# First and last iterations of a two-layer attention pipeline rebuilt, the mask moved behind the projection, new instruction orders

## Chip, cores, metric

The kernel runs on one core of a Trainium2 chip. The metric is the device time of one execution in microseconds (us), lower is better. TensorE is written PE, VectorE DVE, ScalarE ACT, GpSimd POOL, SyncE SP.

## What is computed

For each of 16 batches `x` is 256 x 512 (features x time) and `mask` is one row of 512 values of 0 or 1. All arrays are fp32. Cut to what matters:

```python
def layer0(x, mask):                       # 8 heads of 32
    q = transpose(x) @ Wq.T                # 512 x 256; keys and values are q as well
    logits = (scale * q q^T * cmask + (1 - cmask) * NEG) * rmask
    ctx = softmax(logits) @ q              # a masked query row gets the plain mean of q over time
    return transpose(ctx @ Wo.T)

def layer1(x, emb=mask):                   # 16 heads of 32, rows are the 256 features
    scale, shift = split(emb @ W_emb + b_emb)
    xn = rms_norm(x) * g_norm * (1 + scale) + shift
    q, k, v = xn @ W_qkv;  q, k = rms_norm over each head of 32
    o = softmax(q k^T * 32**-0.5) @ v
    return o + o @ W_out

x = x + layer0(x, mask);  x = x + layer1(x, mask)
```

## The kernel before

Every engine has its own instruction list, written out by hand; semaphores tie the lists. `pipeline` runs i from -1 to 17. Iteration i of every engine works on three batches at once: layer 0 of batch i, layer 1 of batch i-1, the last output steps of batch i-2, and the projection of batch i+1. Iterations -1, 0, 15, 16 and 17 have lists of their own, 1 to 14 share `iteration`. Iterations 2 to 14 have all four parts; below they are called full iterations. The tables `BIG`, `MAXES`, `CONTEXT_TAKEN`, `VISITS` and `SCORES` hold the order in which steps use a PSUM bank, and every wait count is computed from them.

Layer 0 of a batch. SP loads `XB` (x) and `CBM` (the mask on all partitions) in `load_x`. DVE sums x over time (`sums_x`, L1559), POOL multiplies x by the mask (`mask_x`, L1935; in the first batch DVE does, L1554). PE projects in two halves mt (`project0`, L398) into bank PX; ACT copies to `QF` (`take_query`) and rounds to `QHI` (`round_query`); DVE makes the rest `QLO` (`split0`). PE also projects the sums (`project_mean`, L406: 4 matmuls of one column), and ACT scales that to `MEAN` (L1078). SP stacks high and low parts into `A0` and `B0` (`stack0`, 6 DMAs per head, 64 KB each, L2093), so that one matmul gives near-fp32 scores. PE makes scores once to find row maxima (`maxima0`, L422; DVE reduces, L1565), transposes the maxima (`rows0`, L437), ACT copies them and sends them by DMA into row 96 of `B0` (L1092). Then come 32 scores (`score0`, L453), 32 exponentials (L1048), sums over keys on POOL and DVE, values times weights (`values_weighted0`, L480), sums through a matmul with ones (L491), reciprocals, the mean for masked rows (`context0`, L1614), the output matmul (`out0`, L519), residual, RMS norm, transposes (`norm_rows`, L530) and modulation (`modulate`, which needs `AMOD` and `SMOD`).

Layer 1 of a batch. PE projects in four pieces of 4 matmuls (`qk`, L541) through the one bank PX; ACT copies (`take_heads`) and squares (`square_heads`), DVE sums and adds eps, POOL raises to the power -0.5 (`power_heads`, L1960) and multiplies (`norm_heads`, L1967); PE transposes (`heads_rows`, L559), ACT rounds, DVE splits, SP stacks (`stack1`, 6 DMAs per group of heads, 128 KB each), PE and DVE find maxima (`maxima1`, L431 and L1572), all 32 rows are transposed together (`rows1`, L441) and sent by one DMA. The value projection (`values1`, also L541) and 16 steps of scores (`score1`, L467), exponentials (L1055), `values_and_sums1` (L502, L505) and the output (`out1`, L575) follow, and SP stores. `score1` of the first group waits for `row1_in`, the landing of the row of maxima.

Start. ACT waits for WQ and x, then issues nine loads (`loads`), then its first activation. PE computes the modulation for all batches in iteration -1 (`modulation(n)`, L374, 8 calls of 4 matmuls of 16 columns into PO), in pieces between the maxima of batch 0; `WEMB` lies inside the buffer `E` of the exponentials. SP stacks all heads of batch 0.

End. Iteration 16 has only layer 1 of batch 15. PE's four `qk` pieces take turns with ACT's copies of bank PX; the stacks go out on SP alone:

```python
def iteration_16(i):           # SP
    stack1(i, i - 1, 0)
    stack1(i, i - 1, 1)
    stack1(i, i - 1, 2)
    stack1(i, i - 1, 3)
    store(i, i - 2)
```

## Times and profile before

| | us |
|---|---|
| three runs | 1325.32, 1330.34, 1330.52; median 1330.34 |
| profiled execution | 1324.62 |
| its span | 1322.8 |
| PE busy in the span | 1261.4 (95%) |
| DVE / ACT / POOL busy | 1055.8 / 774.6 / 764.4 |

The profiled execution is one further run; its span is from the first to the last instruction, and 1.8 us lie around it. Busy time is the union of an engine's instructions. The granted clock of TensorE has the mean 0.972 over the span; it is either full (2.4 GHz, 1.0) or half (1.2 GHz, 0.5) at a time.

### The profile page before, as it was taken

The page shows a single profiled execution, that of the slowest core. Times are in us where ns is not written, and L with a number is a line of the kernel's source. Part 1 is how long each engine was busy: PE and PEld are TensorE (multiplying, and loading weights), DVE is VectorE, ACT ScalarE, POOL GpSimd, SP SyncE. Part 2 cuts the span into 40 slices and gives each one's busy share as a digit, 9 for nine tenths or more (in the row PEclk, how much of TensorE's full clock was granted, in tenths as well). Part 3 has the DMA queues.
Part 4 walks back from the last instruction along what each step waited for, and adds up shares of the span by engine and source line. Part 5 has one row for each costly group of instructions (what it writes and reads, how often), then busy time and mean ns, then how long its engine had stood idle before and what let it go on. Part 6 is the DMA issues. An engine that isn't in the chain of part 4 may idle for free.

```text
span 1322.8 us, 20986 instructions
## 1 busy us (share of the span) xinstructions
PE 1261.4 (95%) x6896; PEld 597.6 (45%) x6896; DVE 1055.8 (80%) x934; ACT 774.6 (59%) x1377; POOL 764.4 (58%) x389
## 2 busy tenths in 40 slices
PE   6969899999999999999999999999999999999987
PEld 4424444444444454444445444444444444444433
DVE  6756778888887887888788788878888887888654
ACT  1626565665656566565656666565666656566523
POOL 0337467475746747484674748467474856638452
PEclk8859899999999999999999999999999999999999
DMA  8321534525264452626445252634525263441322
GB/s 288 105 65 47 136 105 96 140 54 151 74 148 109 99 138 56 149 72 150 107 107 131 60 147 70 153 104 112 130 60 145 69 156 100 113 110 44 97 59 70
DMA packets 77962, 143.03 MB, mean 108 GB/s; under 512 B 21536, under 2 KB 23072, under 8 KB 77856
## 3 DMA queue, kind: packets, MB, share of 16 engines
q1 hardware_dynamic: 69136, 126.17, 38.1%
q10 hardware_dynamic: 8720, 15.51, 4.0%
q8 instruction: 59, 0.97, 0.3%
q14 instruction: 47, 0.39, 0.1%
HBM read 32.02 MB, written 8.39 MB: 31 GB/s over the span
## 4 chain that ended last, share of the span: by engine, by line
PE 88%; ACT 4%; DVE 2%; issue 2%; SPq 1%; ACTq 1%; POOL 1%; DMA 0%; DVEq 0%
PE PX L541 25%; PE PS L453 11%; PE PO L480 9%; PE PX L575 8%; PE PO L502 5%; PE PS L467 4%; PE PX L398 4%; PE PM L422 4%; PE PX L519 2%; PE PM L491 2%; PE PM L519 2%; PE PM L559 2%; PE PM L431 2%; PE PO L505 2%; ACT E L1055 2%
## 5 line engine op out<-in xcount | busy, mean ns | idle before, releaser
L1048 ACT ACTIVATE E<-PS,KBIAS 128x512 f32<-128x512 f32 x512 | 345.3, 686 | 236.8 <-PE PS L453 221.9
L541 PE MATMUL PX<-WQKV,XNT 128*128 128x512 f32 x768 | 382.4, 602 | 3.4 <-ACT QK L1026 2.1
L1948 POOL TENSOR_TENSOR E<-E 128x1024 f32<-128x1024 f32 x112 | 263.4, 2359 | 160.8 <-PE PO L480 92.9
L1565 DVE TENSOR_REDUCE NM<-PM 128x4 f32<-128x2048 f32 x128 | 291.3, 2276 | 52.3 <-PE PM L422 52.3
L453 PE MATMUL PS<-B,A 97*128 97x512 f32 x512 | 301.7, 624 | 5.3 <-ACT E L1048 4.9
L1978 POOL TENSOR_TENSOR KQLO<-E 128x1024 f32<-128x1024 f32 x64 | 151.2, 2363 | 211.3 <-ACT E L1055 209.5
L1960 POOL TENSOR_TENSOR RQK<-RQK,HALF 128x16 f32<-128x16 f32 x64 | 201.0, 3148 | 28.3 <-DVE RQK L1653 27.5
L1572 DVE TENSOR_REDUCE NM<-PM 128x8 f32<-128x2048 f32 x64 | 146.6, 2291 | 49.1 <-PE PM L431 49.0
L541 PEld LDWEIGHTS PX<-WQKV,XNT 128*128 128x128 f32 x768 | 137.8, 192 | 91.4 <-issue 75.7
L1055 ACT ACTIVATE E<-PS 128x512 f32<-128x512 f32 x256 | 145.3, 596 | 49.0 <-PE PS L467 48.3
L453 PEld LDWEIGHTS PS<-B,A 97*128 97x128 f32 x512 | 95.6, 192 | 148.1 <-issue 123.6
L480 PE MATMUL PO<-E,V 128*32 128x512 f32 x1024 | 139.5, 617 | 0.0
L467 PE MATMUL PS<-B,A 97*128 97x256 f32 x512 | 124.4, 350 | 8.8 <-ACT E L1055 8.2
L1672 DVE RECIPROCAL T<-T 128x256 f32<-128x256 f32 x64 | 111.5, 1742 | 12.4 <-ACT T L1026 12.4
L575 PE MATMUL PX<-WOUT,OT 128*128 128x512 f32 x248 | 120.5, 605 | 0.0
L467 PEld LDWEIGHTS PS<-B,A 97*128 97x128 f32 x512 | 77.2, 188 | 80.2 <-issue 53.1
L1603 DVE RECIPROCAL R<-R 128x256 f32<-128x256 f32 x64 | 109.8, 1736 | 1.1
L1583 DVE TENSOR_TENSOR E<-E 128x1024 f32<-128x1024 f32 x80 | 97.7, 1238 | 11.9 <-ACT E L1048 10.1
L1935 POOL TENSOR_TENSOR XB<-XB,CBM 128x512 f32<-128x512 f32 x30 | 37.8, 1281 | 72.6 <-DVE XS L1559 56.6
L422 PE MATMUL PM<-QHI 32*128 32x512 f32 x512 | 67.1, 513 | 10.5 <-DVE NM L1565 6.9
L1646 DVE TENSOR_REDUCE SSQ<-YSQ 128x16 f32<-128x512 f32 x64 | 42.8, 669 | 40.2 <-ACT YSQ L1116 40.1
L398 PE MATMUL PX<-XB,WQ 128*128 128x512 f32 x128 | 65.6, 637 | 8.0 <-DVE XB L1554 8.0
(84 smaller groups left out, 1408.2 us busy)
## 6 DMA issues: line engine op xcount, KB each, us to landing
A<-QHI SPq DMA_DIRECT2D x256, 64.0 KB, 2.0
B<-QHI SPq DMA_DIRECT2D x256, 64.0 KB, 2.0
A<-KQHI SPq DMA_DIRECT2D x128, 128.0 KB, 2.3
B<-KQHI SPq DMA_DIRECT2D x128, 128.0 KB, 2.4
XB<-x SPq DMA_DIRECT2D x16, 512.0 KB, 3.9
A<-QLO SPq DMA_DIRECT2D x128, 64.0 KB, 2.0
B<-QLO SPq DMA_DIRECT2D x128, 64.0 KB, 2.0
X<-x ACTq DMA_DIRECT2D x16, 512.0 KB, 5.4
```

What stands on the lines that cost most here:

```text
L453: mm(PS[n % 2][:, :], A0[0:97, h, g * P:(g + 1) * P], B0[0:97, h, :], start=True, stop=True).then_inc(score_full, 1)
L467: last = mm(PS[n % 2][:, kb * N1:(kb + 1) * N1], A1[0:97, hq, c, kb * P:(kb + 1) * P], B1[0:97, hq, c, :], start=True, stop=True)
L480: last = mm(PO[h * DH:(h + 1) * DH, :], V0[:, q, g, h * DH:(h + 1) * DH], E[:, probs(seg, i, g), h, :], start=(g == 0), stop=(g == KB0 - 1))
L541: last = mm(PX[:, :], XNT[:, c, t * P:(t + 1) * P], WQKV[:, c, part * DM:(part + 1) * DM], start=(c == 0), stop=(c == 3))
L575: last = mm(bank, OT[:, c, t * P:(t + 1) * P], WOUT[:, c, :], start=(c == 0), stop=(c == 3))
L1048: fn(E[:, probs(seg, i, g), h, :], PS[n % 2][:, :], ACT.Exp, bias=KBIAS[:, g, b:b + 1], scale=SCALE).then_inc(exp_done, 1)
L1055: fn(E[:, probs("C", i, c), h, :], PS[n % 2][:, :], ACT.Exp, scale=SCALE_RAW).then_inc(exp_done, 1)
L1565: v.tensor_reduce(NM0[:, q, :].rearrange("p (h k) -> p h k", k=KB0)[:, :, kb], PM[:, :, :], axis=AX.X, op=ALU.max, negate=True).then_inc(m ...
L1572: v.tensor_reduce(NM1[:, :].rearrange("p (h c a) -> p h c a", c=Q1, a=2)[:, :, c, :], PM[:, :, :].rearrange("p h (a k) -> p h a k", a=2), ...
L1948: g_.tensor_tensor(running(seg, i)[:, heads_, :], running(seg, i)[:, heads_, :], E[:, probs(seg, i, g), heads_, :], ALU.add).then_inc(done, 1)
L1960: g_.tensor_tensor(rqk, rqk, HALF[:, :], ALU.pow).then_inc(rqk_done.sem, 1)
L1978: g_.tensor_tensor(key_sums(c), e[:, :, 0:N1], e[:, :, N1:2 * N1], ALU.add).then_inc(esum_done.sem, 1)
```

## The change

- **Mask after the projection.** x is projected as it is. `take_query` also gives the sum of its input over time (`accum_out` into `QSUM`), which replaces `sums_x` (DVE), `project_mean` (PE) and `mean0` (ACT); the factor 1/512 goes into `CBI` and into NEG. POOL multiplies `QF` by the mask (`mask_query`, two multiplications per batch as before), and `round_query` and the transposes of `values0` wait for it.
- **Start.** ACT issues five small loads and waits for nothing before them. SP issues the large ones: W_emb and W_o behind the first stack, W_qkv and W_out behind the last stack of iteration -1. ACT issues four of the eight stacks of batch 0. `WEMB` has space of its own under `B1` and what follows. The modulation is one block in iteration 0, into PX, between scores; DVE's part of it and `residual_weights` are in iteration 0 too.
- **Full iterations.** All engines but SP get a new order: `qk`, `out1`, `maxima1` and `values1` are cut and spread otherwise, `heads_rows` come earlier, `split0` of the second half and `round_query` of it come at the end, `masked_out` stands behind the fourth `power_heads`.
- **Iteration 15** has new orders; the store comes behind the stacks.
- **Iteration 16.** The odd `qk` pieces go through bank 3 of PM. `norm_heads` is on DVE. ACT issues two of the four stacks, SP the others. The maxima are transposed and sent in two halves (`rows1_half`), four DMAs each, and scores of groups 0 and 1 wait only for the first half.

```diff
-            def project_mean(i, b):
-                big(("mean", 0), i)
-                pe.wait_ge(xs_done.sem, xs_done.at(b))
-                for mt in range(2):
-                    for c in range(2):
-                        last = mm(PX[:, mt:mt + 1], WQ[:, c, mt * P:(mt + 1) * P], XS[:, c:c + 1],
-                                  start=(c == 0), stop=(c == 1))
-                last.then_inc(p0_full.sem, 1)
...
             def project0(i, b, mt):
-                pe.wait_ge(xm_done.sem, xm_done.at(b))
+                pe.wait_ge(xin_in.sem, xin_in.at(b))
...
+            def rows1_half(i, b, j):
+
+                pe.wait_ge(context_taken, CONTEXT_TAKEN.ahead(("n1", j), i))
+                pe.wait_ge(max_done, MAXES.upto(("c", 2 * j + 1), i, QUAD))
+                tp(PO[0:H1, j * P:(j + 1) * P], NM1[:, j * H1:(j + 1) * H1], IDENT[:, :]).then_inc(n1_half[j], 1)
...
             def score1(i, b, c, hq):
...
+                if b == NB - 1:
+                    if u in (0, 8):
+                        pe.wait_ge(row1_half_in[u // 8], 16 * QH)
+                elif u == 0:
...
         @block.scalar
...
-                copy(QF[:, mt, :], PX[:, :]).then_inc(big_taken, 1)
+                fn(QF[:, mt, :], PX[:, :], ACT.Copy, accum_out=QSUM[:, mt, b:b + 1]).then_inc(big_taken, 1)
...
             def round_query(i, b, mt):
-                act.wait_ge(big_taken, BIG.upto(("p0", mt), i))
+                act.wait_ge(masked.sem, masked.at(b, mt + 1))
...
+            def rows1_half(i, b, j):
+                act.wait_ge(n1_half[j], 1)
...
+                copy(NMT1[0:H1, j, :], PO[0:H1, j * P:(j + 1) * P]).then_inc(context_taken, 1)
+                act.wait_ge(context_taken, CONTEXT_TAKEN.upto(("n1", j), i))
+                for h in range(QH):
+                    act.dma_start(B1[96:97, h, 2 * j:2 * j + 2, :].rearrange("p c (k t) -> p (c k) t", t=P).bitcast(F32),
+                                  NMT1[h * QH:(h + 1) * QH, j, :].bitcast(F32)).then_inc(row1_half_in[j], 16)
...
             def loads():
-                act.wait_ge(wq_in.sem, 16)
-                act.wait_ge(xin_in.sem, xin_in.at(0))
...
         @block.gpsimd
...
-            def mask_x(i, b):
+            def mask_query(i, b, mt):
                 pool.wait_ge(cbm_in.sem, cbm_in.at(b))
-                pool.wait_ge(xs_done.sem, xs_done.at(b))
-                for c in range(2):
-                    g_.tensor_tensor(XB[:, c, :], XB[:, c, :], CBM[:, :], ALU.mult).then_inc(xm_done.sem, 1)
+                pool.wait_ge(big_taken, BIG.upto(("p0", mt), i))
+                g_.tensor_tensor(QF[:, mt, :], QF[:, mt, :], CBM[:, :], ALU.mult).then_inc(masked.sem, 1)
...
         @block.sync
...
             def iteration_before(i):
-                stack0(i + 1, 0, 3)
-                stack0(i + 1, 0, 1)
                 stack0(i + 1, 0, 0)
+                load_modulation()
                 load_x(i + 2)
                 stack0(i + 1, 0, 2)
-                stack0(i + 1, 1, 3)
                 stack0(i + 1, 1, 2)
                 stack0(i + 1, 1, 0)
-                stack0(i + 1, 1, 1)
+                load_weights()
...
             def iteration_16(i):
                 stack1(i, i - 1, 0)
-                stack1(i, i - 1, 1)
-                stack1(i, i - 1, 2)
-                stack1(i, i - 1, 3)
                 store(i, i - 2)
+                stack1(i, i - 1, 2)
```

How the rows move is shown at three places. First PE from its first instruction to the third piece of batch 0's scores (PX<-XB,WQ is `project0`, PM<-QHI `maxima0`, PO<-CT,E or PX<-CT,WEMB the modulation, IDENT,NM `rows0`, IDENT,QF `values0`, PS<-B,A the scores). Before:

```order
1 L398 MATMUL PX<-XB,WQ 128x512 x2
2 L422 MATMUL PM<-QHI 128x512 x4
3 L398 MATMUL PX<-XB,WQ 128x512 x2
4 L422 MATMUL PM<-QHI 128x512 x4
5 L374 MATMUL PO<-CT,E 128x16 x12
6 L422 MATMUL PM<-QHI 128x512 x8
7 L374 MATMUL PO<-CT,E 128x16 x4
8 L406 MATMUL PX<-XS,WQ 128x1 x4
9 L437 MATMUL PM<-IDENT,NM 16x128
10 L374 MATMUL PO<-CT,E 128x16 x16
11 L414 MATMUL PM<-IDENT,QF 128x128 x4
12 L453 MATMUL PS<-B,A 128x512 x2
```

Now:

```order
1 L427 MATMUL PX<-XB,WQ 128x512 x4
2 L442 MATMUL PM<-QHI 128x512 x16
3 L457 MATMUL PM<-IDENT,NM 16x128
4 L434 MATMUL PM<-IDENT,QF 128x128 x4
5 L427 MATMUL PX<-XB,WQ 128x512 x2
6 L442 MATMUL PM<-QHI 128x512 x4
7 L479 MATMUL PS<-B,A 128x512 x4
...
15 L479 MATMUL PS<-B,A 128x512 x2
16 L442 MATMUL PM<-QHI 128x512 x4
17 L411 MATMUL PX<-CT,WEMB 128x16 x32
18 L457 MATMUL PM<-IDENT,NM 16x128
```

The 32 modulation matmuls left the stretch ahead of the first score and stand behind the twelfth, and half of batch 1's projection and a piece of maxima stand ahead of the first.

Second PE in a full iteration, from the end of the first quarter of scores to the first `maxima1` (IDENT,QK is `heads_rows`, PM<-KQHI `maxima1`, PX<-WOUT,OT `out1`). Before:

```order
475 L398 MATMUL PX<-XB,WQ 128x512 x2
476 L453 MATMUL PS<-B,A 128x512 x2
477 L559 MATMUL PM<-IDENT,QK 128x128 x8
478 L398 MATMUL PX<-XB,WQ 128x512 x2
479 L453 MATMUL PS<-B,A 128x512
480 L491 MATMUL PM<-E,ONES 32x512 x4
481 L453 MATMUL PS<-B,A 128x512 x2
482 L559 MATMUL PM<-IDENT,QK 128x128 x8
483 L453 MATMUL PS<-B,A 128x512 x2
484 L480 MATMUL PO<-E,V 32x512 x4
485 L406 MATMUL PX<-XS,WQ 128x1 x4
486 L431 MATMUL PM<-KQHI 128x256 x8
```

Now:

```order
477 L427 MATMUL PX<-XB,WQ 128x512 x2
478 L593 MATMUL PM<-IDENT,QK 128x128 x8
479 L479 MATMUL PS<-B,A 128x512 x2
480 L427 MATMUL PX<-XB,WQ 128x512 x2
481 L518 MATMUL PM<-E,ONES 32x512 x4
482 L479 MATMUL PS<-B,A 128x512 x2
483 L593 MATMUL PM<-IDENT,QK 128x128 x8
484 L479 MATMUL PS<-B,A 128x512
485 L507 MATMUL PO<-E,V 32x512 x4
486 L609 MATMUL PX<-WOUT,OT 128x512
487 L479 MATMUL PS<-B,A 128x512
488 L451 MATMUL PM<-KQHI 128x256 x8
```

The row with XS is gone, and both blocks of `heads_rows` stand ahead of scores that they stood behind.

Third ACT in iteration 16, from the rounding of keys and queries to the exponentials of group 1 (NMT are the maxima, V the values). Before:

```order
984 L1132 ACTIVATE KQHI<-PM,GQK 128x512 x4
985 L1026 ACTIVATE V<-PX 128x512
986 L1026 ACTIVATE NMT<-PM 32x128
987 L1100 DMA B<-NMT 1x32x128
988 L1055 ACTIVATE E<-PS 128x512 x6
```

Now:

```order
952 L1184 ACTIVATE KQHI<-PM,GQK 128x512 x4
953 L1098 DMA A<-KQHI 32x1024
...
962 L1098 DMA B<-KQLO 32x1024
963 L1055 ACTIVATE NMT<-PO 16x128
964 L1148 DMA B<-NMT 1x4x128 x4
965 L1055 ACTIVATE V<-PX 128x512
966 L1084 ACTIVATE E<-PS 128x512 x4
967 L1055 ACTIVATE NMT<-PO 16x128
968 L1148 DMA B<-NMT 1x4x128 x4
969 L1084 ACTIVATE E<-PS 128x512 x2
```

Twelve stack DMAs stand ahead of the maxima, and the second half of the maxima, with four DMAs, stands between exponentials.

## Rows read from the trace of the kernel before

**Rows 1.** The page, part 1: engine, busy us (share of the span), instructions.

```profile
PE 1261.4 (95%) x6896; PEld 597.6 (45%) x6896; DVE 1055.8 (80%) x934; ACT 774.6 (59%) x1377; POOL 764.4 (58%) x389
```

**Rows 2.** Busy time by stretch, with granted clock, DMA share, GB/s.

```profile
0.00:35.90 35.90, 22.96 (x97) 16.77 (x98) 20.98 (x17) 4.18 (x7) 0.73 (x7) 0.79 0.85 279
35.90:99.70 63.80, 49.62 (x188) 20.39 (x189) 41.57 (x41) 27.92 (x50) 22.82 (x12) 0.69 0.31 81
99.70:178.60 78.90, 73.86 (x389) 34.66 (x387) 58.47 (x52) 47.49 (x85) 45.40 (x23) 0.92 0.39 94
178.60:1179.30 1000.70, 987.04 (x5559) 467.46 (x5555) 845.06 (x742) 627.74 (x1118) 621.60 (x312) 1.00 0.44 110
1179.30:1252.70 73.40, 70.44 (x398) 32.43 (x395) 54.70 (x50) 45.25 (x79) 46.16 (x22) 1.00 0.31 78
1252.70:1310.90 58.20, 48.72 (x244) 22.33 (x242) 27.46 (x28) 20.87 (x37) 25.98 (x13) 0.94 0.27 64
```

**Rows 3.** Timeline of PE, full iteration: start us, us, instruction, [idle before <-releaser].

```profile
444.58 1.05 PE L406 MATMUL PX<-XS,WQ 128*128 128x1 f32 x8
445.56 0.51 PE L431 MATMUL PM<-KQHI 32*128 32x256 f32 x8
```

**Rows 4.** Timeline of PE near the end of the same iteration.

```profile
479.19 0.50 PE L467 MATMUL PS<-B,A 97*128 97x256 f32 x2 [0.45 <-ACT E L1055]
...
482.52 0.28 PE L437 MATMUL PM<-IDENT,NM 128*16 128x128 f32 x1 [0.29 <-DVE NM L1565]
...
485.05 1.07 PE L502 MATMUL PO<-E,V 128*32 128x256 f32 x16 [0.29 <-ACT T L1026]
```

**Rows 5.** Timeline of POOL in the same iteration: mask, powers, normalised heads.

```profile
425.92 0.62 POOL L1939 TENSOR_SCALAR CBI<-CBI 128x512 f32<-128x512 f32 x1 [0.52 <-DMA CBI<-cond]
...
436.99 3.81 POOL L1960 TENSOR_TENSOR RQK<-RQK,HALF 128x16 f32<-128x16 f32 x1 [0.36 <-DVE RQK L1653]
440.88 1.05 POOL L1967 TENSOR_TENSOR QK<-QK,RQK 128x512 f32<-128x512 f32 x1
```

**Rows 6.** Timeline of PE there: the second block of `heads_rows`.

```profile
441.98 1.09 PE L559 MATMUL PM<-IDENT,QK 128*128 128x128 f32 x8
```

**Rows 7.** Timeline of PE in iteration 1, layer 1 maxima and what follows.

```profile
142.22 0.51 PE L431 MATMUL PM<-KQHI 32*128 32x256 f32 x8 [1.96 <-DVE NM L1572]
...
145.12 0.80 PE L431 MATMUL PM<-KQHI 32*128 32x256 f32 x8 [0.81 <-DVE NM L1572]
...
148.65 1.94 PE L480 MATMUL PO<-E,V 128*32 128x512 f32 x8
```

**Rows 8.** Timeline of PE at the start.

```profile
8.01 3.75 PE L398 MATMUL PX<-XB,WQ 128*128 128x512 f32 x4 [8.01 <-DVE XB L1554]
...
29.26 6.85 PE L374 MATMUL PO<-CT,E 128*128 128x16 f32 x32
...
36.69 1.20 PE L453 MATMUL PS<-B,A 97*128 97x512 f32 x2
```

**Rows 9.** Timeline of ACT at the start (ACTq: its DMA issues).

```profile
12.89 0.60 ACT L1026 ACTIVATE QF<-PX 128x512 f32<-128x512 f32 x1
...
29.80 0.60 ACTq L1092 DMA_DIRECT2D B<-NMT  x1
```

**Rows 10.** Timeline of PE in iteration 16.

```profile
1256.99 3.70 PE L541 MATMUL PX<-WQKV,XNT 128*128 128x512 f32 x8 [0.69 <-ACT QK L1026]
...
1297.18 0.71 PE L467 MATMUL PS<-B,A 97*128 97x256 f32 x4 [0.51 <-issue]
```

**Rows 11.** Timeline of SP's issues in iteration 16, first and last of 24.

```profile
1278.93 0.51 SPq L2093 DMA_DIRECT2D A<-KQHI  x1
...
1294.71 0.59 SPq L2093 DMA_DIRECT2D B<-KQLO  x1
```

**Rows 12.** Timeline of ACT in iteration 16.

```profile
1294.42 0.53 ACTq L1100 DMA_DIRECT2D B<-NMT  x1
```

**Rows 13.** DMA issues over the run: KB each, median us to landing.

```profile
A<-KQHI SPq DMA_DIRECT2D x128, 128.0 KB, 2.3
```

810 lines of the change are left out of this document (425 added, 385 removed), and 23 rows, old and new, of tables (BIG, special).

## Prediction

> **What bounds the kernel now.** I began with busy time on the page: PE is busy for 1261.4 of 1322.8 us, DVE for 1055.8, ACT and POOL for less than 780 [rows 1]. So PE sets the time, and 61.4 us of the span are its idle time. The table of stretches says where they lie [rows 2]: the 13 full iterations take 1000.7 us, 77.0 each, and PE idles for 13.7 us in all of them, 1.05 each, at a clock of 1.00. The start idles for 12.9, iteration 0 for 14.2, iteration 1 for 5.0, iteration 15 for 3.0, iteration 16 for 9.5. The same rows hold a second loss. A mean clock of 0.69 over iteration 0's 63.8 us is 2 x 0.31 x 63.8 = 40 us at half clock; 0.92 in iteration 1 is 12.6 us, 0.94 in iteration 16 is 7.0 us. Work takes twice as long there, so these cost some 20, 6.3 and 3.5 us.
>
> Then I took PE's timeline for each place that the diff touches. What PE still loses in a full iteration are waits of 0.45, 0.29 and 0.29 us near its end [rows 4]; all else there is work that only fewer instructions can shorten.
>
> **Full iterations, mask after the projection.** Removed on PE: the matmuls of the sums. From their start at 444.58 to the next instruction at 445.56 they hold PE for 0.98 us [rows 3]; PE is the bound, so all of it is gained: **-0.98** each. The sums on DVE, the scaling on ACT and the two masks on POOL go, shrink or stay, on engines with 20 to 42% to spare [rows 1], so I price them at nothing; their cover is PE's work.
>
> **Full iterations, the new order.** It can at most take away the three waits, 1.03 us; a wait can also be hidden in what rows count as busy, so I allow 0.3 more: -1.3. What may come in their place lies on POOL. Before, `masked_out` (0.62 us at 425.92) stood ahead of the powers; the fourth power ran at 436.99 for 3.81 us, the last `norm_heads` from 440.88 to 441.93 [rows 5], and PE began the `heads_rows` that need it at 441.98 [rows 6]. There was no slack. Now 0.62 us of `masked_out` stand between that power and that norm, and PE has less to do before it. So a wait of 0.6 to 1.0 us is born ahead of the second `heads_rows`; I take 1.0. Reorder -1.3, new wait +1.0, sum **-0.3**. With the mask that is -1.3 for each iteration, 13 x 1.3 = **-17**. Ends: -26 (no new wait, 2.0 each beside rounding) and 0 (waits eat what the matmuls gave).
>
> **Start and iteration 0.** Before, PE started at 8.01, released by DVE's masking [rows 8]. Two products of that shape cost 1.05 each on POOL [rows 5], so PE starts some 2 to 3 us earlier. The row of maxima of the first head was issued at 29.80 on ACT [rows 9]; with a landing of 2.3 as the stacks have [rows 13] it was there at 32.1. The first score came only at 36.69, for 16 matmuls of the modulation, which hold PE for 6.85 us from 29.26, stood ahead of it [rows 8]. ACT now has about six issues each of four stacks ahead of that row, 0.6 us each, some 14 us in all, which begin after `round_query`; its own first activation was at 12.89 [rows 9] and moves forward by the 2 to 3 us. That leaves the row at about 30 and the first score at about 32: -4.6. But all 32 modulation matmuls now lie inside iteration 0: 13.7 us at half clock (twice the 6.85), 6.9 at full; I take 10.3. They fill idle time, of which iteration 0 has 14.2 [rows 2]; I count 4 of it. And half of batch 1's projection (3.75 us at half clock [rows 8]) is done before the first score, in time that was idle. -4.6 + 10.3 - 4 - 3.8 = **-2**. Ends: -9 (the modulation wholly in idle time and at full clock) and +8 (nothing filled, clock as before).
>
> **Iteration 1.** PE waited 1.96 and 0.81 for DVE's maxima of layer 1, and the block behind them, 8 passes of 512 columns, took 1.94 us at half clock [rows 7]. The maxima are now spread between other work. The two waits are 2.8; of the 6.3 us that half clock costs, a share goes too. I take **-4**, ends -8 and 0.
>
> **Iteration 15.** It idles for 3.0 us [rows 2]; new orders and the lacking L406 can give half of that: **-1.5**, ends -3 and +1.
>
> **Iteration 16.** Three `qk` pieces wait 0.69 us each for ACT's copy of the one bank [rows 10]; with a second bank these go: -2.1. The 24 stack issues run from 1278.93 to 1295.3 on SP alone [rows 11], 16.4 us, 0.68 each. The maxima row was issued at 1294.42 [rows 12]; it lands 2.3 later and releases the first score at 1297.18 [rows 10]. Now ACT issues 12 stacks ahead of it, from 1276.8 on: 12 x 0.62 = 7.4, then a copy, four DMAs of 0.6, 2.3 of landing, and a remainder for waits: about 1289.6, 7.6 earlier. Given back: the second half's four DMAs (2.4) and its copy stand between exponentials on ACT, and value matmuls that used to fill the wait are left over behind it; 3.1 together. So **-4.5**, ends -2 and -8.5.
>
> Here a rule of the Trainium skill can be set against the rows. The rows say that issue is the bound there: 24 issues fill 16.4 us, and each stack lands 2.3 us after its issue. The Trainium skill (DMA: Bandwidth & Descriptors, Issuing engines are not separate DMA queues) says that DMAs from several engines share the same 16 DMA engines, and issuing from more than one saves only issue time. By rows, 24 x 128 KB in 8.2 us would be 384 GB/s, while the start moved 279 GB/s at a share of 0.85 [rows 2], so at most 328; by that rule the stacks take 9.6 us, and iteration 16 gives 1.4 us less.
>
> **Sum.** -17 - 2 - 4 - 1.5 - 4.5 = -29 against the profiled execution's 1324.62: 1295.6. The runs shown have a median 5.7 us above it, with one of them at 1325.3. I put the forecast a little under half of that above the sum: **1298**, against a median of 1330.3, -2.4%.
>
> **Rivals.**
>
> *A, the chain through POOL is the bound of a full iteration.* For: no slack between norm and `heads_rows` [rows 5, 6], and POOL's powers are long. If the wait is 2.3 us instead of 1.0, the full iterations give nothing: 1324.6 - 12 = 1312.6, and with the allowance for the median 1315. Against: POOL is busy for 58% only [rows 1]. Chance 0.18.
>
> *B, more is hidden than rows show.* Waits that look like work go as well, full iterations take 75 us (-26), and the clock stays full in iteration 1 and most of iteration 0 (-17 instead of -6, from the 26 us that half clock costs): 1324.6 - 26 - 17 - 6 = 1276, with the allowance 1278. For: half clock in iterations 0 and 1 begins behind idle time. Chance 0.12.
>
> *C, slower: a gap in each full iteration that takes the clock down.* In iteration 1, waits of 1.96 and 0.81 close together were followed by half clock: 8 passes took 1.94 us [rows 7] where 0.97 would do. If the new order's `heads_rows` wait and a wait for maxima behind it come to 2 or 3 us within a few us, each full iteration may lose half of some 10 us, as iteration 1 lost 6.3. That is +5 x 13 = 65, less the 29: 1360. [...] Chance 0.04. The Trainium skill (TensorE: Matmul & The Clock Gate, HAM oscillation — how this bites in real kernels) describes this case: a gap that comes once per loop lowers the clock anew each time. Iteration 1's rows agree with it; no full iteration's do.
>
> *D, the change is of no effect where it aims.* The DMAs bound start and end (share 0.85 in the start [rows 2]), the waits in full iterations move instead of going, and only some 5 us of the 12.7 of removed matmuls are left: 1320 to 1325. Chance 0.03.
>
> **How the numbers follow.** Forecast 0.63, A 0.18, B 0.12, C 0.04, D 0.03. The range is the forecast's own, whose ends I add half-way, since they don't fall together: 1281 to 1316. It takes in A, and leaves out most of B, C and D. About 0.5%, 6.6 us, is what a measurement of this kernel can tell from no change. Slower by more: C, 0.04. Within: D and the tail of A, 0.05. Faster: the rest, 0.91.
>
> **What would show it.** Full iterations of 75.7 us; the waits of rows 4 gone; a wait for POOL's QK of 0.6 to 1.0 us ahead of the second `heads_rows`. The first score at about 32 us, and iteration 0 about 2 us longer than before in itself, measured from there. No wait over 1 us for NM in iteration 1. In iteration 16, `qk` without waits and the first score some 22 us behind the end of the last `qk` piece instead of 27.7 [rows 10]. I am wrong if the full iterations stay at 77 us (A), if their clock is below 1.00 (C), or if the gain sits in the first and last iterations.

## Result and the profile after

| | us |
|---|---|
| changed kernel, six runs | 1315.93 to 1320.96; median 1316.75 |
| kernel before, six runs beside it | 1324.55 to 1331.37; median 1330.34 |
| ratio | 0.9923, 95% interval 0.9898 to 0.9948 |
| profiled execution, changed kernel | 1315.93 (span 1313.8) |

The change gives 13.6 us by the medians, and 8.7 between the two profiled executions (1324.62 and 1315.93). Forecast were 1298 and a range from 1281 to 1316, so the time lies just outside it, and the gain is less than half of the forecast one. One execution of a kernel below (mod_late) took 1421.4 us at a mean granted clock of 0.83 and is left out of its median and ratio.

The page of the changed kernel, part 1, answers to [rows 1]:

```profile
PE 1238.3 (94%) x6769; PEld 578.4 (44%) x6769; DVE 1040.7 (79%) x920; ACT 768.5 (58%) x1394; POOL 770.5 (59%) x387
```

PE is busy for 23 us less, DVE for 15 less, but the span is only 9 us shorter: idle time of PE has grown by 14 us. Where, the table by stretch says. For both kernels the stretches end at the same events: the first score of layer 0 of batches 0, 1, 2 and 15, and the first score of iteration 16. Columns as in [rows 2]: stretch, its length, busy time of PE, weight loads, DVE, ACT and POOL, granted clock, DMA share, GB/s. Before:

```profile
0.00:36.70 36.70, 23.76 (x102) 17.57 (x102) 21.53 (x21) 4.18 (x7) 0.73 (x7) 0.79 0.84 275
36.70:103.40 66.70, 52.52 (x195) 22.12 (x194) 43.14 (x41) 28.29 (x50) 24.05 (x14) 0.68 0.32 82
103.40:180.80 77.40, 72.36 (x388) 33.63 (x387) 58.52 (x50) 47.72 (x85) 46.31 (x24) 0.93 0.40 100
180.80:1180.30 999.50, 985.84 (x5548) 466.47 (x5546) 843.89 (x741) 627.74 (x1118) 620.42 (x313) 1.00 0.44 110
1180.30:1297.20 116.90, 106.29 (x526) 47.40 (x524) 76.16 (x74) 54.64 (x95) 63.45 (x31) 0.97 0.32 78
1297.20:1322.80 25.60, 20.61 (x146) 10.38 (x146) 12.59 (x10) 12.08 (x22) 9.48 (x4) 1.00 0.09 34
```

The changed kernel:

```profile
0.00:37.20 37.20, 14.27 (x37) 5.13 (x38) 18.86 (x11) 5.47 (x11) 4.52 (x10) 0.72 0.72 200
37.20:112.10 74.90, 57.31 (x241) 29.00 (x241) 48.13 (x46) 27.36 (x48) 20.13 (x12) 0.71 0.29 97
112.10:188.30 76.20, 70.64 (x381) 32.30 (x380) 55.88 (x48) 47.08 (x86) 46.77 (x24) 0.93 0.41 96
188.30:1171.90 983.60, 970.67 (x5444) 452.80 (x5443) 826.25 (x729) 621.83 (x1131) 628.47 (x313) 1.00 0.45 112
1171.90:1284.10 112.20, 100.42 (x520) 46.09 (x518) 78.80 (x79) 54.43 (x95) 61.15 (x27) 0.98 0.35 88
1284.10:1313.80 29.70, 25.01 (x153) 13.07 (x153) 12.79 (x10) 12.29 (x23) 9.48 (x4) 0.90 0.05 19
```

The 13 full iterations took 999.5 and take 983.6 us, 15.9 less. Iteration 1 is 1.2 shorter. Start and iteration 0 together took 103.4 and take 112.1, 8.7 more. The end, from batch 15's first score of layer 0 on, took 142.5 and takes 141.9, 0.6 less; inside it the first score of iteration 16 comes 4.7 us earlier and the stretch behind it is 4.1 us longer. The sum is the 9.0 us by which the span is shorter.

**Full iterations.** The summary of PE's waits over these 13 iterations (releaser, us in total, times, longest), before:

```profile
PE PS L467 <- ACT E L1055: 5.9, 13, 0.5
PE PO L502 <- ACT T L1026: 3.9, 13, 0.3
PE PM L437 <- DVE NM L1565: 3.8, 13, 0.3
```

and of the changed kernel:

```profile
PE PM L593 <- POOL QK L2013: 10.6, 13, 0.8
```

The three waits of [rows 4] are gone (for ACT's E 0.7 us in total are left), and one new wait of 0.8 us each stands ahead of the second `heads_rows`. POOL's timeline in one iteration shows what makes it, where [rows 5] had the power and the norm back to back:

```profile
441.84 3.81 POOL L2006 TENSOR_TENSOR RQK<-RQK,HALF 128x16 f32<-128x16 f32 x1 [0.33 <-DVE RQK L1693]
445.63 0.62 POOL L1985 TENSOR_SCALAR CBI<-CBI 128x512 f32<-128x512 f32 x1
446.22 1.04 POOL L2013 TENSOR_TENSOR QK<-QK,RQK 128x512 f32<-128x512 f32 x1
```

**Start.** PE begins at 5.66, not at 8.01 [rows 8], as forecast. ACT issues the row of maxima at 29.42 [rows 9]. Then, on PE's timeline:

```profile
31.30 3.78 PE L427 MATMUL PX<-XB,WQ 128*128 128x512 f32 x4 [0.72 <-DMA XB<-x]
35.01 0.80 PE L442 MATMUL PM<-QHI 32*128 32x512 f32 x4
37.21 1.19 PE L479 MATMUL PS<-B,A 97*128 97x512 f32 x2 [1.40 <-issue]
...
50.58 11.11 PE L411 MATMUL PX<-CT,WEMB 128*128 128x16 f32 x64
...
88.17 1.94 PE L518 MATMUL PM<-E,ONES 128*32 128x512 f32 x8 [5.41 <-DVE E L1623]
```

and among the DMA issues between 12 and 45 us (KB each, median us to landing):

```profile
WEMB<-w_emb SPq DMA_DIRECT2D x1, 2048.0 KB, 10.3
A<-QHI ACTq DMA_DIRECT2D x8, 64.0 KB, 6.5
XB<-x SPq DMA_DIRECT2D x1, 512.0 KB, 13.2
B<-NMT ACTq DMA_DIRECT2D x1, 8.0 KB, 7.7
```

The row of 8 KB needed 7.7 us to land (3.6 before) and x of batch 1 13.2 us. SP issued the 2 MB of W_emb at 16.76, ahead of both. W_emb had landed at 27.1, before the row was issued; what was still under way then were x and the stacks, which took 6.5 us to land on ACT's queue and 10.6 on SP's. The modulation, 32 matmuls of 16 columns, holds PE for 11.1 us between scores.

DVE's part of the modulation costs more than its own time. It stands ahead of a reciprocal that POOL needs, and POOL's sums over keys are what DVE's last sums, and so PE at 88.17, wait for:

```profile
73.79 5.54 DVE L1597 TENSOR_SCALAR AMOD<-AMOD,GN 128x16 f32<-128x16 f32 x4
81.06 1.29 POOL L2000 TENSOR_TENSOR QK<-QK,R 128x512 f32<-128x512 f32 x1 [1.90 <-DVE R L1643]
```

**End.** ACT in iteration 16, from its last stack issues on:

```profile
1267.43 0.55 ACTq L1098 DMA_DIRECT2D A<-KQHI  x1
...
1277.54 0.27 ACT L1055 ACTIVATE NMT<-PO 16x128 fp32r<-16x128 f32 x1 [11.07 <-issue]
1277.83 3.00 ACTq L1148 DMA_DIRECT2D B<-NMT  x4
1280.94 0.60 ACT L1055 ACTIVATE V<-PX 128x512 f32<-128x512 f32 x1 [3.14 <-issue]
```

Its 12 issues take from 1267.43 to 1277.44, 0.83 each, where SP's took 0.68 in [rows 11] and I had put 0.62. PE had the maxima of the first half transposed at 1273.7; ACT's copy of them had to wait until 1277.54. PE stood idle for 6.89 us ahead of its first score at 1284.07, fell to half clock, and still had half of the value projection left, which it then made between scores.

### The profile page after: what moved, and what is told of

It is laid out like the page before. It is cut to its first block, busy times and chain, and to the rows that moved or that the text cites. A ratio compares the mean times of both kernels' runs of the same rounds, so it can differ in the third digit from the quotient of the medians.

```text
span 1313.8 us, 20726 instructions
## 1 busy us (share of the span) xinstructions
PE 1238.3 (94%) x6769; PEld 578.4 (44%) x6769; DVE 1040.7 (79%) x920; ACT 768.5 (58%) x1394; POOL 770.5 (59%) x387
## 4 chain that ended last, share of the span: by engine, by line
PE 76%; POOL 8%; issue 4%; DVE 4%; SPq 3%; ACT 2%; DMA 2%; ACTq 1%; POOLq 0%; DVEq 0%
PE PX L575 24%; PE PS L479 8%; PE PO L507 7%; PE PX L609 6%; PE PS L496 6%; POOL RQK L2006 5%; PE PO L529 5%; PE PM L442 4%; SPq L2162 2%; PE PX L546 2%; PE PM L546 2%; PE PO L532 2%; PE PM L451 2%; DMA XB<-x 1%; PE PM L434 1%
## 5 line engine op out<-in xcount | busy, mean ns | idle before, releaser
L1077 ACT ACTIVATE E<-PS,KBIAS 128x512 f32<-128x512 f32 x512 | 340.3, 686 | 193.5 <-PE PS L479 148.8
L575 PE MATMUL PX<-WQKV,XNT 128*128 128x512 f32 x752 | 375.0, 602 | 0.1
L479 PE MATMUL PS<-B,A 97*128 97x512 f32 x512 | 286.6, 598 | 5.3 <-ACT E L1077 3.6
L2006 POOL TENSOR_TENSOR RQK<-RQK,HALF 128x16 f32<-128x16 f32 x64 | 213.6, 3344 | 89.9 <-DVE RQK L1693 89.8
L575 PEld LDWEIGHTS PX<-WQKV,XNT 128*128 128x128 f32 x752 | 133.9, 191 | 96.0 <-issue 86.3
L1612 DVE TENSOR_REDUCE NM<-PM 128x8 f32<-128x2048 f32 x64 | 146.5, 2289 | 37.2 <-PE PM L451 37.2
L496 PE MATMUL PS<-B,A 97*128 97x256 f32 x512 | 138.0, 376 | 9.1 <-issue 6.9
L609 PE MATMUL PX<-WOUT,OT 128*128 128x512 f32 x248 | 125.7, 600 | 0.1
L1623 DVE TENSOR_TENSOR E<-E 128x1024 f32<-128x1024 f32 x80 | 101.8, 1274 | 19.8 <-ACT E L1077 16.6
L1055 ACT ACTIVATE QK<-PX 128x512 f32<-128x512 f32 x62 | 37.1, 599 | 79.3 <-PE PX L575 79.3
L1686 DVE TENSOR_REDUCE SSQ<-YSQ 128x16 f32<-128x512 f32 x64 | 43.7, 683 | 37.9 <-ACT YSQ L1168 37.8
```

Of the source, the lines that this page charges most:

```text
L479: mm(PS[n % 2][:, :], A0[0:97, h, g * P:(g + 1) * P], B0[0:97, h, :], start=True, stop=True).then_inc(score_full, 1)
L496: last = mm(PS[n % 2][:, kb * N1:(kb + 1) * N1], A1[0:97, hq, c, kb * P:(kb + 1) * P], B1[0:97, hq, c, :], start=True, stop=True)
L575: last = mm(bank, XNT[:, c, t * P:(t + 1) * P], WQKV[:, c, part * DM:(part + 1) * DM], start=(c == 0), stop=(c == 3))
L609: last = mm(bank, OT[:, c, t * P:(t + 1) * P], WOUT[:, c, :], start=(c == 0), stop=(c == 3))
L1077: fn(E[:, probs(seg, i, g), h, :], PS[n % 2][:, :], ACT.Exp, bias=KBIAS[:, g, b:b + 1], scale=SCALE).then_inc(exp_done, 1)
L1612: v.tensor_reduce(maxima_rows(b)[:, c // 2, c % 2, :, :], PM[:, :, :].rearrange("p h (a k) -> p h a k", a=2), axis=AX.X, op=ALU.max, negat ...
```

## Experiments

All are edits to the changed kernel and compute what it computes; `sums_back` and `no_slack` add matmuls whose result is overwritten. Stage times of the profiled executions, in us, with the same events as above (full: mean of 13 iterations):

| kernel | first score | iteration 0 | 1 | full | to first score of 16 | tail | median | ratio to before |
|---|---|---|---|---|---|---|---|---|
| before | 36.7 | 66.7 | 77.4 | 76.88 | 116.9 | 25.6 | 1330.3 | |
| changed | 37.2 | 74.9 | 76.2 | 75.67 | 112.1 | 29.7 | 1316.8 | 0.9923 |
| loads_late | 36.8 | 75.7 | 77.0 | 75.55 | 112.2 | 31.1 | 1315.4 | 0.9920 |
| mod_late | 38.3 | 72.7 | 77.6 | 75.56 | 112.0 | 29.6 | 1314.2 | 0.9916 |
| mod_early | 37.0 | 64.2 | 76.4 | 75.57 | 111.9 | 31.1 | 1305.0 | 0.9842 |
| mask_last | 39.1 | 78.6 | 78.6 | 76.31 | 112.9 | 29.6 | 1328.7 | 1.0025 |
| mask_mid | 36.6 | 77.4 | 77.1 | 75.36 | 111.7 | 30.3 | 1315.6 | 0.9932 |
| sums_back | 37.3 | 78.8 | 76.7 | 75.60 | 112.9 | 29.8 | 1319.8 | 0.9951 |
| rows_first | 37.0 | 78.6 | 76.8 | 75.62 | 108.2 | 36.1 | 1318.1 | 0.9946 |
| end_split | 37.2 | 78.8 | 76.5 | 75.56 | 107.4 | 35.9 | 1316.4 | 0.9940 |
| end_sp | 38.2 | 75.3 | 76.3 | 75.58 | 106.9 | 35.8 | 1318.7 | 0.9945 |
| best1 | 37.9 | 64.6 | 76.4 | 75.43 | 112.8 | 29.4 | 1303.8 | 0.9827 |
| best2 | 34.6 | 63.9 | 76.3 | 75.39 | 112.9 | 31.1 | 1300.2 | 0.9808 |
| best3 | 34.7 | 63.8 | 76.2 | 75.39 | 111.9 | 30.0 | 1300.5 | 0.9815 |
| best4 | 34.0 | 63.3 | 76.4 | 75.37 | 112.0 | 30.4 | 1300.4 | 0.9824 |
| no_slack | 39.7 | 63.5 | 77.4 | 75.48 | 111.7 | 29.1 | 1305.9 | 0.9865 |

The intervals of the ratios are 0.002 to 0.004 to either side. Each ratio is against runs of the kernel before on the same chip, whose medians were 1322.7 to 1330.3. Iteration 0 has a spread of its own: six kernels have the code of the changed one there, and it took 74.9 to 78.8 us, longer where the clock came up later (mean granted clock 0.71 in the changed kernel, 0.65 in mask_mid at 77.4 us, 0.63 in end_split at 78.8). The tail of the kernels without an edit of the end took 29.6 to 31.1. So a few us in these columns, or in whole kernels that differ elsewhere, say nothing; the column of the edited stage does.

### The start

**loads_late**: W_emb and W_o behind the stacks.

```diff
                 stack0(i + 1, 0, 0)
-                load_modulation()
                 load_x(i + 2)
...
                 stack0(i + 1, 1, 0)
+                load_modulation()
                 load_weights()
```

> Edit to the changed kernel: SP issues W_emb (2 MB) and W_o behind all of its stacks of batch 0, ahead of W_qkv, not behind the first stack. Theory (DMA traffic): in the changed kernel the row of maxima, issued at 29.42, lands only at 37.1, and x of batch 1 needs 13.2 us, since W_emb's 2 MB are in the queues ahead of them; then here x lands within 6 us of its issue, the row within 3 us of 29.4, and the first score is held only by PE's own order (projection and maxima ahead of it): 35.2 instead of 37.2. Rival (the order on PE and ACT sets the start, not the traffic): first score stays at 37.2 +- 0.3. In both, the modulation at about 50 may now wait for W_emb, by 0 to 3 us. Whole kernel: theory -2 us, rival 0.

The landing of x fell from 13.2 to 5.2 us and the row's from 7.7 to 5.6. The first score came only 0.4 us earlier, which by itself is the rival's number. But in this execution the work at the start ran 1.8 us later (the fourth maxima at 23.20 for 21.41, behind a projection at half clock), and the row was issued at 31.15 for 29.42. In both kernels the row's landing releases the first score, and the 2.1 us that it lands faster are the size that the theory gave. Its 3 us for the row did not come true: here W_emb was issued 0.7 us ahead of the row. With W_emb issued at 5.7 us (mod_early and best2 below) the row lands in 3.3 and 2.9. The whole kernel's 1.4 us are inside the noise. So traffic was a part of what the start lost, some 2 us by these landings; no whole-kernel time shows it.

**mod_late**: the modulation block at PE's wait for DVE at the end of iteration 0.

```diff
                 maxima0(i, i, 1, 3)
-                modulation(i)
                 rows0(i, i, 1)
...
                 values_weighted0("B", i, 1, 3)
+                modulation(i)
                 weights_summed0("B", i, 1)
```

> Edit to the changed kernel: the block of 32 modulation matmuls in iteration 0 stands ahead of the last sums over keys, where PE waits 5.4 us for DVE, and not ahead of the second rows of maxima; DVE's part moves with it, the bank PX is used in that order. Theory: the 11.1 us at half clock between scores were wholly on the path, and half clock lasted until 66 us because of them; here the block fills the 5.4 us wait, and from the first score (37.2) to the second batch's first score it takes 63 to 68 us instead of 74.9; whole kernel -7 to -12 us. Rival (the stretch is bound by DVE's maxima and ACT's exponentials, and PE's clock matters little): -0 to -3 us.

PE's timeline:

```profile
76.00 11.08 PE L411 MATMUL PX<-CT,WEMB 128*128 128x16 f32 x64
```

The block took 11.08 us there as well. But the wait of 5.4 us that it was to fill was not there in that size: with the block gone from between the scores, DVE's sums were ready at 77.08,

```profile
74.98 2.10 DVE L1623 TENSOR_TENSOR E<-E 128x1024 f32<-128x1024 f32 x1 [4.00 <-ACT E L1077]
```

so PE would have waited for about 1 us at 76, and the block ran on until 87. Iteration 0 took 72.7 us: 2 to 6 less than with the block between scores, where the theory had 63 to 68 in all. The whole kernel, 2.6 us faster by the medians and inside the noise, is in the rival's range of 0 to 3. The rival's reason, that PE's work matters little in this stretch, falls with the next run.

**mod_early**: the block back ahead of the first score, in the waits between maxima; ACT issues W_emb once x is there, and DVE's part moves with it.

```diff
+                act.wait_ge(wq_in.sem, 16)
+                act.wait_ge(xin_in.sem, xin_in.at(0))
+                act.dma_start(WEMB[:, :, :], ...
...
             def iteration_before(i):
...
                 maxima0(i, i + 1, 0, 1)
+                modulation(i, 0)
                 maxima0(i, i + 1, 0, 2)
+                modulation(i, 1, 2)
                 maxima0(i, i + 1, 0, 3)
+                modulation(i, 3, 4)
                 rows0(i, i + 1, 0)
+                modulation(i, 5, 6, 7)
```

> Edit to the changed kernel: the modulation goes back ahead of the first score, in the waits between and behind the first maxima; W_emb is issued by ACT as soon as x and W_q are there. Theory (the modulation block between scores costs its own 11 us and keeps the clock at half): first score at 37 +- 1.5, from there to the second batch's first score 60 to 66 us instead of 74.9; whole kernel -8 to -14 us against the changed kernel. Rival (start bound by traffic: 2 MB more ahead of stacks and row push the first score back): first score at 40 or later, whole kernel -5 or less.

Iteration 0 falls from 74.9 to 64.2 us, and the first score stays where it was, 37.0. The whole kernel gains 11.7 us on the changed one (ratio 0.9842, interval 0.9818 to 0.9865). At the start the block costs the first score nothing: PE's waits for DVE's maxima, 2.4 us four times in the changed kernel, and the 4.5 behind them now hold it.

```profile
18.12 0.80 PE L443 MATMUL PM<-QHI 32*128 32x512 f32 x4 [0.60 <-DVE NM L1612]
18.84 3.60 PE L411 MATMUL PX<-CT,WEMB 128*128 128x16 f32 x16
...
52.46 0.28 PE L458 MATMUL PM<-IDENT,NM 128*16 128x128 f32 x1 [2.40 <-DVE NM L1612]
...
76.59 1.46 PE L519 MATMUL PM<-E,ONES 128*32 128x512 f32 x8 [3.50 <-DVE E L1630]
```

The last two rows say what the block's place was worth. Where it had stood between scores, PE now waits 2.40 us for DVE's maxima, so the block had hidden that much; and PE's wait for DVE's last sums is 3.50 and not 5.41, as DVE's part of the modulation no longer holds up POOL there. 11.1 - 2.4 + 1.9 is 10.6, and iteration 0 is 10.7 shorter. The theory holds for the block's own length; its part on the clock has little in it (mean granted clock of iteration 0: 0.73 for 0.71). The traffic rival, which had the first score at 40, falls: the row lands in 3.3 us and the first score waits for PE's own order. **best2** is best1 (mod_early, mask_mid and an edit of the end, below) with one more piece at the start:

```diff
                 values0(i, i, 0)
-                project0(i, i + 1, 0)
                 maxima0(i, i, 1, 0)
                 score0("A", i, i, 0, 0, 0)
...
                 score0("A", i, i, 0, 0, 3)
+                project0(i, i + 1, 0)
```

> best1, and batch 1's first projection half stands behind the first four scores instead of ahead of the first one (its copy on ACT likewise). Theory: with the modulation back at the start the first score at 37.0 waits for PE's own order alone (projection 3.4 us); the row is there about 33.5, so the first score comes at 34 to 35 and the whole kernel gains 1 to 3 us on best1. Rival (iteration 0 is bound by DVE's maxima and POOL behind it, the projection only moves): first score earlier, but the second batch's first score at the same time, 0 +- 1.

The first score comes at 34.6 for 37.9 in best1, and iteration 0 isn't longer for it. The medians differ by 3.6 us. So PE's own order was the second thing ahead of the first score: in the changed kernel the projection and a maxima piece had PE until 35.8 whatever the row did.

### Full iterations

**mask_last**: `masked_out` behind the fourth norm.

```diff
                     power_heads(i, i - 1, 3)
-                if l0:
-                    masked_out(i, i)
-                if l1:
                     norm_heads(i, i - 1, 3)
+                if l0:
+                    masked_out(i, i)
```

> Edit to the changed kernel, full iterations only: masked_out on POOL stands behind the fourth norm_heads and not between the fourth power and it. Theory: the wait of 0.80 us ahead of the second heads_rows is made by this 0.62 us; it falls to 0.2 and each full iteration from 75.67 to 75.05 us; whole kernel -8 us. Rival: PE or another wait takes it back further on, full iterations stay above 75.5, whole kernel -0 to -2.

It made the kernel 12 us slower than the changed one. PE's waits over the full iterations:

```profile
PE PM L451 <- DVE KQLO L1712: 12.1, 13, 0.9
PE PM L593 <- POOL QK L2013: 4.4, 13, 0.4
```

The wait for QK falls to 0.3 us, near the expected 0.2, and a wait for KQLO of 0.9 takes its place. The full iterations take 8.4 us more in all (983.6 to 992.0), the greater part of the 12. DVE's timeline says why:

```profile
457.93 0.69 DVE L1637 SCALAR_TENSOR_TENSOR R<-CBI,PM 128x512 f32<-128x512 f32 x1 [1.82 <-POOL CBI L1985]
458.66 1.75 DVE L1643 RECIPROCAL R<-R 128x256 f32<-128x256 f32 x1
460.33 1.31 DVE L1712 SCALAR_TENSOR_TENSOR KQLO<-PM,GQK,KQHI 128x512 fp32r<-128x512 f32 x2
```

DVE's `take_sums0` waits for `masked_out`, and the last two splits of layer 1 are queued behind it. **mask_mid** therefore moves it the other way, where POOL waits 0.33 us:

```diff
                     norm_heads(i, i - 1, 2)
-                    power_heads(i, i - 1, 3)
                 if l0:
                     masked_out(i, i)
                 if l1:
+                    power_heads(i, i - 1, 3)
                     norm_heads(i, i - 1, 3)
```

> Edit to the changed kernel, full iterations: masked_out stands between the third norm_heads and the fourth power, where POOL waits 0.33 us, not behind that power. The kernel mask_last showed that DVE's sums wait for masked_out and stand ahead of two splits, so that it can't go later. Theory: 0.33 of its 0.62 us are hidden, the wait of 0.80 ahead of heads_rows falls to about 0.46 and the iteration from 75.6 to 75.3; whole kernel -4. Rival (the first norms or the power itself delay another chain by as much): 75.6, whole kernel 0.

75.36 us, where kernels with the changed one's full iterations took 75.55 to 75.67: 0.2 to 0.3 for each iteration, near the expected 0.3, though the wait itself reads 0.68 and not 0.46. By the whole kernel's runs the 4 us can't be told from noise.

**sums_back**: the removed matmuls alone, put back.

```diff
                 big(("p0", mt), i)
+                if mt == 1:
+                    for m in range(2):
+                        for c in range(2):
+                            mm(PX[:, m:m + 1], WQ[:, c, m * P:(m + 1) * P], XB[:, c, 0:1],
+                               start=(c == 0), stop=(c == 1))
```

> The changed kernel with four matmuls of one column per batch put back into the projection (their result is overwritten and not used): the price of the removed ones alone, without their DVE and ACT work. Forecast's term: 0.98 us of PE in each full iteration, 75.67 to 76.6, whole kernel +14 to +16. Rival (they fit into the wait of 0.80 ahead of heads_rows and other gaps): 75.7 to 76.0, whole kernel +0 to +5; then the order, and not the mask, gave most of the 1.3.

The rival came true. The full iterations by the table of stretches, 13 of them, with the sums and (above) without:

```profile
192.80:1175.70 982.90, 980.67 (x5550) 465.12 (x5548) 824.79 (x729) 621.12 (x1131) 628.20 (x313) 1.00 0.46 113
```

PE is busy for 10.0 us more, 0.77 for each iteration, and the stretch isn't longer: the wait for POOL's QK is gone from the trace, so the new wait of 0.8 us took the matmuls in. Against the kernel before, PE has the same work in these iterations: 76.88 to 75.60, of which 11.4 us over 13 iterations are idle time that went, and 5.2 us are busy time (985.84 to 980.67) that no row shows as a wait. What differs is the order of all engines, and with it the mask's new place and the sums that DVE and ACT no longer make (DVE is busy for 19 us less). No run separates these, so that the order gave the 1.28 us is not shown. **no_slack** asks the same of a kernel with a shorter wait:

> best4 with the four matmuls of one column per batch put back as in the kernel sums_back. There they cost nothing in a full iteration (75.60 for 75.67), since PE waited 0.80 us for POOL just behind them. Here that wait is about 0.46. Theory (the removed 0.98 us were gained, and lost again to the wait for POOL): the sums now cost 0.98 less the wait, +0.5 us in each full iteration, 75.4 to 75.9, whole kernel +6 to +8 with iterations 1 and 15. Rival (the iteration is bound by a chain outside PE, and PE's work is free at this size): 75.4, whole kernel +0 to +2.

75.48 for 75.37, an excess of 0.11 where I expected 0.5. Two numbers were wrong in that: the sums cost 0.76 (9.9 us of busy time over 13), and the wait was 0.68. Their difference is 0.08, which agrees with the theory's mechanism. But kernels with the same full iterations (mask_mid, best1 to best4) differ by 0.07 among themselves, so this run hardly tells the theory from its rival, which had 75.4. The whole kernel's 5.5 us look like the expected 6 to 8 and are something else: the first score came at 39.7 for 34.0. There the sums (1.8 us at half clock) stand ahead of the second half of the first projection, which ran at half clock too (3.6 us for 2.0), and the row, issued 4.3 us later and behind W_qkv, took 5.9 us to land.

### The end

**rows_first**: on ACT the first half of the row ahead of the second stack.

```diff
-                stack1(i, i - 1, 3)
                 stack1(i, i - 1, 1)
                 rows1_half(i, i - 1, 0)
+                stack1(i, i - 1, 3)
                 values1(i, i - 1, 0)
```

> Edit to the changed kernel, iteration 16 only: ACT issues one stack, then the first half of the row of maxima, then its second stack. Theory: the first score at 1284.1 waits for the row, which stood behind 10.0 us of stack issues on ACT; its maxima were there at 1273.7, so here the row is issued from 1274 to 1276.5, lands at 1279 and the first score comes 4 to 5 us earlier; whole kernel -3 to -5 us. Rival (the stacks' own landing or the DMA traffic holds the first score): first score less than 1 us earlier, whole kernel 0.

The first score does come 3.9 us earlier, so ACT's queue held it. But the tail grew by 6.4: the stack now kept the values' copy and the exponentials waiting (the copy at 1287.52, behind six issues from 1281.67 on), and the whole kernel gained nothing.

**end_split** (ACT one stack, SP three) and **end_sp** (SP all four, the store behind them):

```diff
             def iteration_16(i):
                 stack1(i, i - 1, 0)
-                store(i, i - 2)
+                stack1(i, i - 1, 1)
                 stack1(i, i - 1, 2)
+                stack1(i, i - 1, 3)
+                store(i, i - 2)
```

> Edit to the changed kernel, iteration 16: ACT issues one stack, then the first half of the row; SP issues the three others, and the store behind them. The kernel rows_first had its first score 4 us earlier, but ACT's second stack then stood ahead of values and exponentials. Theory (ACT's issues are what costs): first score 4 us earlier than with two stacks on ACT (108 us behind batch 15's first score of layer 0, for 112) and a tail of 30 us; whole kernel -4 us. Rival (the stacks' landing decides): the first scores of the last heads wait for SP's third stack, tail 34 or more, whole kernel 0.

> Edit to the changed kernel, iteration 16: all four stacks on SP, ACT issues none. Theory (issue time on one queue is hidden, since each head's first score needs its own stack alone): first score at 107 to 108 us, tail 31 to 33 us, whole kernel -1 to -4 us. Rival (the second queue is what gives the gain of the end): the fourth head waits until about 1285, tail 36 or more, whole kernel +2 or more.

In both the first score is 5 us earlier and the tail 6 us longer. PE's timeline of end_sp:

```profile
1279.27 0.71 PE L496 MATMUL PS<-B,A 97*128 97x256 f32 x4 [1.67 <-issue]
...
1285.17 0.80 PE L496 MATMUL PS<-B,A 97*128 97x256 f32 x2 [3.52 <-DMA B<-KQLO]
```

The first scores of the last heads wait for their stacks, as the rival had said in both cases. The last two parts together are 142.7 us with one queue and 141.8 with two: in these executions the second queue is worth 1 us, and that is less than what these two parts differ by in kernels with the same end (141.6 to 143.3).

**best1**, the sum of mod_early and mask_mid, with the value projection ahead of the first score:

```diff
                 maxima1(i, i - 1, 3)
+                values1(i, 1, 0, 1, 2, 3)
                 score1(i, i - 1, 0, 0)
...
-                rows1_half(i, i - 1, 0)
                 values1(i, i - 1, 0)
+                rows1_half(i, i - 1, 0)
```

> The edits of mod_early and mask_mid together, and one more in iteration 16: ACT copies the first value projection ahead of the first half of the row, and PE makes the four pieces of the second value projection ahead of the first score. In the changed kernel PE stood idle 6.9 us there, fell to half clock for it, and did those four pieces (5.5 us, half of them at half clock) between scores. Theory: mod_early's 1305 less 3 for mask_mid; end: first score 0.7 us later, tail 26 to 27 us for 29.7 to 31.1; together -6 against mod_early, about 1299. Rival (the tail is paced by exponentials, and PE's work between scores was hidden): tail unchanged, end +0.7, about 1303.

The whole kernel's 1303.8 us are the rival's number: the first score came 0.9 later than in mod_early, and the tail stayed near 30.

**best3**, the second half of the row on SP, with best2's start and without best1's end:

```diff
-                for h in range(QH):
-                    act.dma_start(B1[96:97, h, 2 * j:2 * j + 2, :]...
+            def row1_half(i, j):
+                sp.wait_ge(context_taken, CONTEXT_TAKEN.upto(("n1", j), i))
+                for h in range(QH):
+                    sp.dma_start(B1[96:97, h, 2 * j:2 * j + 2, :]...
```

> The edits of mod_early, mask_mid and best2's order at the start, without best1's edit of the end; instead the second half of the row of maxima in iteration 16 is issued by SP, which is idle by then, and not by ACT between exponentials. Theory: in the changed kernel's tail the four issues hold ACT for 2.4 us behind the fourth exponential, and exponentials pace the tail; the tail falls from 29.7 to about 27.3 us, the last two parts together from 141.8 to 139.5; whole kernel 1297 to 1298. Rival (the row's later landing or the stacks pace the tail): last two parts 141.5 to 143, whole kernel as best2, 1300.

**best4**, both:

> best3 with best1's edit of the end too: value projection ahead of the first score, and the second half of the row on SP. Each of the two alone left the tail at 29 to 31 us. Theory (two covers over one another: exponentials waited for ACT's issues in the one, for PE's projection at half clock in the other): only together they shorten it, to 26 to 27 us, the last two parts together from 141.8 to 139.5 or less; whole kernel -2.5 to -4 against best3's 1300.5. Rival (a third thing paces the tail, such as the row's landing or the stacks of the last heads): 141.5 to 143 again, whole kernel as best3.

None of them shortened the tail: 29.4, 30.0, 30.4 us. Each removed what it was made to remove. What came next, in best1 on ACT, in best4 on PE:

```profile
1275.39 2.42 ACTq L1150 DMA_DIRECT2D B<-NMT  x4
1277.91 1.08 ACT L1086 ACTIVATE E<-PS 128x512 f32<-128x512 f32 x2 [2.55 <-issue]
```

```profile
1272.27 1.22 PE L497 MATMUL PS<-B,A 97*128 97x256 f32 x4 [2.01 <-DMA B<-NMT]
1273.42 1.94 PE L530 MATMUL PO<-E,V 128*32 128x256 f32 x16
```

In best1 four issues held ACT for 2.4 us and the exponentials behind it; in best4 PE waited 2.0 us for the second half of the row itself and went to half clock again. By the times the rivals are right in best3 and best4: a third cause paces the tail. I read it as the chain of each half (maxima, their transposing, four issues and a landing), as long as the waits that were taken away; no run tests that.

## Why the prediction was wrong

Set against its own terms, in us:

| term | forecast | measured |
|---|---|---|
| full iterations | -17 | -15.9 |
| start and iteration 0 | -2 (-9 to +8) | +8.7 |
| iteration 1 | -4 | -1.2 |
| iteration 15 | -1.5 | -1.8 |
| iteration 16 | -4.5 | +1.2 |
| sum | -29 | -9.0 |

Iterations 15 and 16 are divided at the first `qk` matmul of iteration 16 (1252.7 us before, 1242.5 now).

**Full iterations: right, with its parts.** The forecast was -0.98 for the sums, -1.3 for the order, +1.0 for a wait born ahead of `heads_rows`. Measured: -0.77, -1.28 (sums_back against before), and a wait of 0.80. The sum, 1.2 each, hides that the removed matmuls gave nothing here: their time became idle time in front of POOL's norm. All of the gain came with the rest of the change, the new orders and the work that DVE and ACT lost, which no run takes apart. The prediction had that work at nothing, as PE is the bound; whether it was is open. Rival A had the mechanism, but not the size that would have decided.

**Start and iteration 0: the failed step.** The forecast was -4.6 for the first score, +10.3 for the modulation, -4 of it in idle time, -3.8 for the projection done early. Measured: the first score came 0.5 us later; the modulation costs 10.7 (mod_early against the changed kernel; more against the slower executions of the same iteration 0); without it iteration 0 is 2.5 us shorter than before (64.2 for 66.7), where the early projection had been put at 3.8. That makes the +8.7. Two steps of the forecast are wrong here. "The first score at about 32": I gave the row the 2.3 us that stacks need to land in mid-kernel [rows 13], with W_emb's 2 MB issued ahead of x and most of the stacks, and it took 7.7; and I called the projection half and the maxima piece work in idle time, while by the order shown ahead of the prediction they stand in front of the first score. loads_late and best2 put the two at some 2 and 3 us. "They fill idle time, I count 4 of it": most of iteration 0's idle time lies at its end, behind DVE, and not where the block stands. There it hid 2.4 us, and DVE's part of the modulation, which the prediction did not price, gave 1.9 of that back through POOL. The upper end of this term, +8, nearly took it in; the range of the whole missed it because I added the ends at half. (By that same rule the lower end is 1285, not the 1281 that was written.)

**Iteration 1.** I took the waits for maxima to be spread away. They are still there, 0.80, 1.74 and 0.34 for the 1.96 and 0.81 of [rows 7]:

```profile
148.79 0.51 PE L451 MATMUL PM<-KQHI 32*128 32x256 f32 x8 [0.80 <-DVE NM L1612]
151.70 0.51 PE L451 MATMUL PM<-KQHI 32*128 32x256 f32 x8 [1.74 <-DVE NM L1612]
154.61 0.80 PE L451 MATMUL PM<-KQHI 32*128 32x256 f32 x8 [0.34 <-DVE NM L1612]
155.34 1.94 PE L507 MATMUL PO<-E,V 128*32 128x512 f32 x8
```

and the block behind them runs at half clock, 1.94 us, as before. In iteration 1 there is no `out1` yet to fill the places between the maxima that the new order keeps for it.

**The end.** Iteration 15 came out as forecast. The `qk` waits of iteration 16 went, also as forecast (2.1). Its first score came 2.9 us earlier, counted from the first `qk` matmul, where the forecast had 7.6; behind the last `qk` piece it stands 26.1 us and not the 22 that were named as the sign. The mis-sized terms: ACT's 12 issues took 10.0 us and not 7.4, the four of the row 3.0 and not 2.4, the landing 3.2 and not 2.3. What is given back was 4.1, not 3.1. So the iteration became 1.2 us longer instead of 4.5 shorter. The second queue, which most of the 7.6 rested on, is worth 0.9 us by end_sp against the changed kernel. The Trainium skill (DMA: Bandwidth & Descriptors, Issuing engines are not separate DMA queues) says that a second issuing engine saves sequencer time alone. By that rule the prediction had 1.4 us less for this end. Measured are 5.7 us less, so the rule points the right way and is too small to account for it.

Rival C did not come: with 0.8 us of idle time in one place, the clock of the full iterations stayed at 1.00.

**A version that beats both.** mod_early, mask_mid and best2's order together, with best1's end: best2, 1300.2 us, ratio to before 0.9808 (0.9780 to 0.9835); best3 and best4 are equal to it within their intervals. That is near the forecast's own time, though by the ratio it is -1.9% where the forecast had -2.4%: the kernel before ran at 1325.5 beside best2 and at 1330.3 beside the changed one. Most of it comes from undoing the part of the change that moved the modulation.

Still open: what the order alone gave in the full iterations, apart from the work that DVE and ACT lost; what the two halves of the row are worth (a version with the row in one piece, on two stack queues, was not run), and why the clock came up at different times in iteration 0 in kernels with the same code there.
